# Softmax sums of four heads in one group inside the values, divisors spread by small transfers, output a step later

## What is computed

```python
xn = layernorm(x)                                   # x: 8 x 512 x 128, float32
qkv = xn @ W_qkv + b_qkv                            # 16 heads of 64
attention = softmax(q k^T / sqrt(64))               # per sample and head, 512 x 512
attn = (attention @ v).reshape(n, l, 1024) @ W_out + b_out
# gated recurrence over the 8 samples: f, i = sigmoid(...), g = tanh(...), c = f*c + i*g
h = tanh(xn @ wo.T + c_final @ uo.T + bo)           # c_final is the same for all samples
out = x + attn + h
```

## Time and profile before

| | before |
|---|---|
| runs | 881.68 / 883.38 / 883.47 us |
| the profiled execution | 882.6 us, its span 880.8 us |
| TensorE busy | 856.5 us (97%) |
| VectorE busy | 562.0 us (64%) |
| ScalarE busy | 450.5 us (51%) |
| GpSimd busy | 570.0 us (65%) |
| chain that ended last | TensorE 93%, VectorE 4%, ScalarE 2% |

### The profile page before, as it was taken

One profiled execution on the slowest core, in us unless ns is written; L12 is line 12 of the kernel. 1 busy time (PEld: TensorE's weight loads), 2 busy tenths in 40 slices (PEclk: granted clock), 3 DMA queues, 4 the chain that ended last, 5 costly groups with the idle time before them and its releaser, 6 DMA issues.

```text
span 880.8 us, 14963 instructions
## 1 busy us (share of the span) xinstructions
PE 856.5 (97%) x5431; PEld 541.2 (61%) x5431; DVE 562.0 (64%) x743; ACT 450.5 (51%) x585; POOL 570.0 (65%) x299
## 2 busy tenths in 40 slices
PE   6989999999999999999999999999999999999998
PEld 3655565556666566666666566666666566666553
DVE  6775766656777477755776477755777476755722
ACT  6456465455555255555555255554555255554530
POOL 4637584466777377766777377775777477775764
PEclk9999999999999999999999999999999999999999
DMA  8000000000100010000100010000100010000000
GB/s 239 1 1 1 25 1 1 13 1 6 33 1 13 0 36 0 13 0 0 36 0 12 0 36 0 12 0 0 36 0 12 0 36 0 13 1 1 13 13 12
DMA packets 18636, 13.75 MB, mean 16 GB/s; under 512 B 1299, under 2 KB 16177, under 8 KB 18609
## 3 DMA queue, kind: packets, MB, share of 16 engines
q1 hardware_dynamic: 18560, 13.37, 4.9%
q10 hardware_dynamic: 48, 0.02, 0.0%
HBM read 6.83 MB, written 2.10 MB: 10 GB/s over the span
## 4 chain that ended last, share of the span: by engine, by line
PE 93%; DVE 4%; ACT 2%; issue 1%; DMA 0%; ACTq 0%
PE st L799 20%; PE pv L815 13%; PE misc L815 13%; PE st L732 9%; PE mx L780 8%; PE st L807 6%; PE mx L831 6%; PE mx L825 6%; PE misc L715 3%; PE pv L732 2%; PE misc L732 2%; DVE NM L553 2%; PE pv L715 1%; PE mx L715 1%; ACT probs L387 1%; PE st L696 1%
## 5 line engine op out<-in xcount | busy, mean ns | idle before, releaser
L553 DVE TENSOR_REDUCE NM<-mx 128x2 f32<-128x1024 f32 x256 | 313.9, 1226 | 157.2 <-PE mx L780 157.2
L387 ACT ACTIVATE probs<-st 128x1024 f32<-128x1024 f32 x256 | 256.9, 1027 | 71.5 <-PE st L807 64.5
L272 POOL TENSOR_TENSOR AT<-AT,RD 128x512 f32<-128x512 f32 x63 | 80.7, 1281 | 204.1 <-DVE RD L571 145.9
L280 POOL TENSOR_TENSOR PSUMK<-probs 128x1024 f32<-128x1024 f32 x64 | 153.5, 2398 | 56.8 <-ACT probs L387 56.8
L286 POOL TENSOR_TENSOR PSUMK<-PSUMK,probs 128x1024 f32<-128x1024 f32 x64 | 152.9, 2390 | 6.0
L293 POOL TENSOR_TENSOR PSUMK<-PSUMK,probs 128x1024 f32<-128x1024 f32 x64 | 152.7, 2386 | 6.1
L815 PE MATMUL misc<-probs,VALL 128*64 128x512 f32 x512 | 129.2, 593 | 2.2 <-DVE DL L518 2.2
L815 PE MATMUL pv<-probs,VALL 128*64 128x512 f32 x512 | 125.2, 609 | 0.2 <-DVE RES L524 0.2
L780 PE MATMUL mx<-KH,QH 64*128 64x512 f32 x512 | 106.7, 412 | 7.1 <-DVE NM L553 6.5
L799 PE MATMUL st<-QH,KH 64*128 64x512 f32 x512 | 104.8, 404 | 0.6 <-ACT probs L387 0.6
L799 PE MATMUL st<-QL,KH 64*128 64x512 f32 x512 | 101.7, 392 | 0.0
(11 more groups left out here) (175 smaller groups left out, 1234.2 us busy)
## 6 DMA issues: line engine op xcount, KB each, us to landing
XSH<-XH SPq DMA_DIRECT2D x8, 256.0 KB, 2.4
XSL<-XL SPq DMA_DIRECT2D x8, 256.0 KB, 2.4
RES<-in_L_attn_data_dram SPq DMA_DIRECT2D x8, 256.0 KB, 2.8
out_dram<-RES SPq DMA_DIRECT2D x8, 256.0 KB, 2.3
probs<-in_L_attn_W_qkv_dram SPq DMA_DIRECT2D x3, 512.0 KB, 5.3
AT<-in_L_attn_data_dram SPq DMA_DIRECT2D x2, 512.0 KB, 6.9
MROW<-TM SPq DMA_DIRECT2D x62, 4.0 KB
AT<-in_L_attn_data_dram SPq DMA_DIRECT2D x1, 768.0 KB, 8.1
```

What stands on the lines that cost most here:

```text
L280: nc.gpsimd.tensor_tensor(PSUMK[:, s % 2, :, :], e[:, :, 0, :], e[:, :, 1, :], ALU.add).then_inc(sum_part, 1)
L387: nc.scalar.activation(probs[:, s % 2, :, u, :], st[:, u % 2, :, :], ACT.Exp, scale=SCALE).then_inc(exp_done, 1)
L553: nc.vector.tensor_reduce(NM[:, 0:4 * TB].rearrange("p (h a b) -> p h a b", h=2, a=2)[:, :, s % 2, b], mx[:, :, :], AX.X, ALU.max, negate= ...
```

## The change

- **Four heads as one group.** In merged stretches (stretch 3 of batch 0, all of batches 1 to 6, stretches 0 to 2 of batch 7) the two calls of `sums` go. In their place `four_sums` runs in the middle of the second pair's values: four products of 32 columns each at column positions 0, 32, 64, 96, all into the bank `st[:, 1, 1, :]`. Before it TensorE waits for `k_lo`. The next stretch's `scores(1)`, which writes that bank, waits for `four_turned`.
- **Divisors.** VectorE turns the group once and takes one reciprocal (`invert_four`). At the head of the next stretch SP spreads the reciprocals over the partitions by six small transfers (`spread_divisors`), and at that stretch's end VectorE fills RD with one transpose per pair (`fill_divisors`), behind the copy of the maxima (`take_max`), in stretch 1 ahead of it.
- **Normalisation** on GpSimd comes one stretch later, both pairs together. The first two pairs of a batch are evacuated into a new tile PV2 in the meantime.
- **Output a step later.** `project_out` and `join` move from stretch 0 to stretch 1, `turn_out`, `finish` and the output's transfer from stretch 1 to stretch 2. `recurrence(3)` stays in stretch 0.
- **The end.** Stretch 3 of batch 7 keeps separate sums; GpSimd does the normalisations of stretch 2 between the sums of its two pairs, and the last output projection is cut in pairs 0 to 3, 4 and 5, 6, 7.

```diff
+            def spread_divisors(n, j):
+
+                sp.wait_ge(four_inverted, fours(n, j) - 1)
+                sp.sem_inc(passed_sp, 1)
+                for a in range(2):
+                    for to, of, count in ((0, 0, 32), (32, 0, 64), (96, 32, 32)):
+                        sp.dma_start(RX[to:to + count, a, :],
+                                     R4[HD * a + of:HD * a + of + count, :]).then_inc(d_r, 16)
...
                 for j in range(STRETCHES):
+                    if not first:
+                        spread_divisors(n, j)
...
-                    if j == 1 and not first:
+                    if j == 2 and not first:
                         sp.wait_ge(out_done, n)
...
                     for k in range(2):
-                        first_sum(t + k, s + k)
+                        first_sum(n, j, t + k, s + k, first)
                         second_sum(t + k, s + k)
                         third_sum(t + k, s + k)
...
+                        if last and j == 3 and k == 0:
+                            normalise(n, t - 2, s - 2)
+                            normalise(n, t - 1, s - 1)
+                    if (first and j < 3) or (last and j == 3):
+                        normalise(n, t, s, first)
+                    elif not first:
+                        normalise(n, t - 2, s - 2)
+                        normalise(n, t - 1, s - 1)
...
+            def invert_four(n, j):
+
+                dve.wait_ge(four_done, fours(n, j))
+                nc.vector.transpose(SD[:, :], st[:, 1, 1, :]).then_inc(four_turned, 1)
+                dve.wait_ge(four_turned, fours(n, j))
+                nc.vector.reciprocal(R4[:, :], SD[:, :].rearrange("p (c j) -> p c j", j=32)[:, :, 0]).then_inc(four_inverted, 1)
+
+            def fill_divisors(n, j, t, a):
+
+                dve.wait_ge(d_r, 96 * (fours(n, j) - 1))
+                dve.wait_ge(norm_done, t - 3 + a)
+                nc.vector.transpose(RD[:, a, :].rearrange("p (c j) -> p c j", j=32),
+                                    RX[:, a, :].unsqueeze(2).to_broadcast([P, L // 32, 32])).then_inc(rd_done, 1)
...
-                    if j == 0 and not first:
+                    if not first and j != 1 and coming:
+                        take_max(STRETCHES * n + j + 1)
+                    if not first:
+                        for a in range(2):
+                            fill_divisors(n, j, t, a)
+                    if j == 1 and not first:
                         join(n - 1)
-                    if j == 1 and not first:
+                    if j == 2 and not first:
                         finish(n - 1)
-                    if coming:
+                    if first or j == 1:
                         take_max(STRETCHES * n + j + 1)
...
+            def four_sums(t):
+
+                pe.wait_ge(sum_done, t + 2)
+                for a in range(2):
+                    for h in range(2):
+                        g = 32 * (2 * a + h)
+                        last = nc.tensor.matmul(st[g:g + 32, 1, 1, :], ones[:, 0:32], PSUMK[:, a, h, :], start=True,
+                                                stop=True, tile_position=(0, g))
+                last.then_inc(four_done, 1)
...
                         staged = 32 * n + 64
+                        pe.wait_ge(four_turned, fours(n, j) - 1)
                         scores(n, t, s, 1)
...
                         recurrence(3, n - 1, h_done, N)
+                    if j == 1 and not first:
                         pe.wait_ge(red_done, 4 * (t + 4))
                         pe.wait_ge(norm_done, 8 * n)
                         project_out(mx[:, 1, :])
-                    if j == 1 and not first:
-                        pe.wait_ge(v_evac, 6 + t)
+                    if j == 2 and not first:
+                        pe.wait_ge(v_evac, 6 + t) if ahead else pe.wait_ge(pv_evac, t)
                         turn_out(n - 1)
...
-                    elif j == 1:
+                    elif j == 2:
                         pe.wait_ge(out_done, n)
...
                     pe.wait_ge(exp_done, 4 * t + 8)
-                    if coming:
+                    if merged:
+                        values(n, t + 1, s + 1, (0, 1))
+                        if ahead:
+                            pe.wait_ge(k_lo, t + 6)
+                        four_sums(t)
+                        values(n, t + 1, s + 1, (2, 3))
```

More of the change, by code:

```diff
@@ L65, in build_block @@
         RD = sb("RD", [P, 2, L])
+        SD = sb("SD", [P, L])
+        R4 = sb("R4", [P, L // 32])
+        RX = sb("RX", [P, 2, L // 32])
+        PV2 = sb("PV2", [P, 2, L])
         AT = sb("AT", [P, PAIRS, L])
@@ L142, in build_block @@
         sum_part, sum_done, norm_done, last_norm = sem("sum_part"), sem("sum_done"), sem("norm_done"), sem("last_norm")
-        d_m = sem("d_m")
+        d_m, d_r = sem("d_m"), sem("d_r")
+        four_done, four_turned, four_inverted = sem("four_done"), sem("four_turned"), sem("four_inverted")
         d_xs, d_res, out_rows = sem("d_xs"), sem("d_res"), sem("out_rows")
@@ L149, in wait, with fours, unnormalised @@
                 eng.wait_ge(s, value)
+        def fours(n, j):
+            return STRETCHES * n + j - 2
+        def unnormalised(first, s):
+            return AT[:, s % PAIRS, :] if first or s % PAIRS >= 2 else PV2[:, s % PAIRS, :]
         def placed(n, j):
@@ L266, in _, with normalise, first_sum @@
             standardise(1)
-            def normalise(t, s):
+            def normalise(n, t, s, first=False):
                 pool.wait_ge(rd_done, t + 1)
                 pool.wait_ge(pv_evac, t + 1)
-                nc.gpsimd.tensor_tensor(AT[:, s % PAIRS, :], AT[:, s % PAIRS, :], RD[:, s % 2, :],
+                if not first and s % PAIRS == 0:
+                    pool.wait_ge(o_done, n)
+                nc.gpsimd.tensor_tensor(AT[:, s % PAIRS, :], unnormalised(first, s), RD[:, s % 2, :],
                                         ALU.mult).then_inc(norm_done, 1)
-            def first_sum(t, s):
+            def first_sum(n, j, t, s, first):
                 pool.wait_ge(exp_done, 4 * t + 2)
-                wait(pool, den_done, t - 1)
+                if first:
+                    wait(pool, den_done, t - 1)
+                else:
+                    pool.wait_ge(four_done, fours(n, j) - 1)
                 e = probs[:, s % 2, :, :, :]
@@ L298, in step @@
                     s, t = 2 * j, 8 * n + 2 * j
-                    if not (first and j == 0):
-                        normalise(t - 1, s - 1)
+                    if first and j > 0:
+                        normalise(n, t - 1, s - 1, True)
                     for k in range(2):
-                        first_sum(t + k, s + k)
+                        first_sum(n, j, t + k, s + k, first)
                         second_sum(t + k, s + k)
@@ L374, in evac_pv @@
                 act.wait_ge(pv_done, t + 1)
[L375 to L379, removed]
+                start = isinstance(n, int) and n == 0
+                if start:
+                    act.wait_ge(xt_done, s % PAIRS + 1)
+                elif s in (0, 1):
+                    act.wait_ge(norm_done, t - 7)
+                elif s == 2:
+                    act.wait_ge(o_done, n)
+                nc.scalar.copy(unnormalised(start, s), value_banks[s % 2]).then_inc(pv_evac, 1)
             def exps(t, s, u):
@@ L560, in take_max, with divisors @@
                 nc.vector.tensor_copy(TM[:, :], mx[0:4 * TB, 0, 0:P]).then_inc(tm_done, 1)
-            def divisors(t, s, source):
+            def divisors(t, s, source, count):
                 r = RD[:, s % 2, :]
-                dve.wait_ge(den_done, t + 1)
+                dve.wait_ge(den_done, count)
                 wait(dve, norm_done, t - 1)
                 nc.vector.transpose(r, source).then_inc(den_used, 1)
-                dve.wait_ge(den_used, t + 1)
+                dve.wait_ge(den_used, count)
                 nc.vector.reciprocal(R16[:, :], r.rearrange("p (c j) -> p c j", j=32)[:, :, 0]).then_inc(r16_done, 1)
-                dve.wait_ge(r16_done, t + 1)
+                dve.wait_ge(r16_done, count)
                 nc.vector.transpose(r.rearrange("p (c j) -> p c j", j=32),
                                     R16[:, :].unsqueeze(2).to_broadcast([P, L // 32, 32])).then_inc(rd_done, 1)
+            def invert_four(n, j):
[8 more added lines that the diff above has]
+                                    RX[:, a, :].unsqueeze(2).to_broadcast([P, L // 32, 32])).then_inc(rd_done, 1)
             def join(n, last=False):
@@ L678, in step @@
                         lo_state(s + 2)
-                    divisors(t, s, mx[:, 1, :])
-                    divisors(t + 1, s + 1, mx[:, 0, :] if coming else st[:, 0, 0, :])
+                    if first and j < 3:
+                        divisors(t, s, mx[:, 1, :], t + 1)
+                        divisors(t + 1, s + 1, mx[:, 0, :], t + 2)
+                    elif last and j == 3:
```

(23 more changed lines are left out.)

3 lines of the change are left out of this document (1 added, 2 removed).

## The result

| | before | after |
|---|---|---|
| runs, median (lowest to highest) | 883.42 us (881.68 to 885.71) | 892.13 us (891.88 to 892.39) |
| span of the profiled execution | 880.8 us | 890.5 us |
| TensorE busy | 856.5 us | 846.6 us |
| VectorE busy | 562.0 us | 529.0 us |

The ratio is 1.0097, 95% interval 1.0074 to 1.0120: slower by about 1%. TensorE has 9.9 us less to do, and the span is 9.7 us longer, so its idle time grew by some 20 us.

What follows compares the result with a forecast made beforehand. TensorE was taken as the bound, busy 856.5 of 880.8 us. Terms -16.0 + 9.8 + 11.4 + 0.9 + 0.6 = +6.7 us gave 890.0 us; likeliest range 884.5 to 897.2, 8 in 10 from 879.5 to 901.

Steps and rivals of the forecast that it cites:

- The sums and the group: Merged stretches: one group for two sums saves 0.59 us (bounds 0.33 and 0.80), 27 times, -16.0 us.
- Both choices between far bounds: Group on TensorE: 0.86 us streaming (bounds 0.86 and 1.71) and 0.13 us per change of tile size (0.03 to 0.26).
- the cap: TensorE's moving operand at 614 GB/s would make the group 1.71 us; the prediction set 1,220 GB/s from the trace against it.
- The output projection: Stretch 1, batches 1 to 7: the projection waits 1.4 us for VectorE's last reduction, +9.8 us.
- The output's finish: Stretch 2: second values wait 1.9 us for finish in batches 1 to 6, +11.4 us; in batch 7 +0.9 us.
- The last stretch: End of batch 7: GpSimd's two normalisations between its chains of sums delay its last sum, +0.6 us.
- Edits at nothing: VectorE's turn and reciprocal, the k_lo wait, GpSimd's earlier sum, small transfers, later normalisations and divisors: priced at no cost.
- A sign that did not come: Sign of being right: TensorE's busy time down by some 20 us with the span longer.
- The first two: Rivals on the group: tiles take turns in pairs, 913 us, chance 0.10; change of tile size free, 883 us, chance 0.11.
- The third: Rival in stretch 2: the wait for out_done does not arise, 9.5 us less, 880.6 us; chance 0.09.
- the fourth: Rival: idle time in the 14 new waits lowers the granted clock, 22 us, 912 us; chance 0.05.
- the forecast of 6.7: Whole kernel: sum of all priced terms, +6.7 us against the kernel before.

Runs made afterwards that it cites:

- b1: The kernel before with each of its 64 calls of sums made on four tiles of 32 columns instead of two of 64: 899.44 us, ratio 1.0180.
- e5: The changed kernel with the eight records of each group issued twice in a row: 915.09 us, ratio 1.0369.
- e2: The changed kernel with recurrence(3) and its tanh moved from stretch 0 to stretch 1, ahead of the output projection: 878.44 us, ratio 0.9941.
- e1: The changed kernel with finish in stretch 2 put first, ahead of the copy of the maxima and the fills: 881.31 us, ratio 0.9977.
- e4: The changed kernel with finish in stretch 2 behind the copy of the maxima and ahead of the two fills: 882.53 us, ratio 0.9989.
- e8: The changed kernel with recurrence(3) moved ahead of the output projection in stretch 1 and finish between the two projections' low halves: 868.63 us, ratio 0.9820.
- after_again: The changed kernel timed once more, with no edit, beside the kernel before: 890.67 us, ratio 1.0078.

## Why the prediction was right, point by point

- **The sums and the group.** Forecast 0.59 us saved per group, measured 0.58. Both choices between far bounds held: side by side (b1, e5), 0.27 us for two changes of form where 0.26 were taken (1.71 - 0.86 - 0.58; 0.25 to 0.3 in b1). The 614 GB/s that the Trainium skill (SBUF — State Buffer, the table of paths) gives the moving operand stand there for bf16; for these float32 streams they are no cap: the group streams 8 x 128 x 512 x 4 bytes in 0.99 us, 2,100 GB/s. The prediction's own 1,220 GB/s against the cap was weaker than it looked: it counts both passes of each product, and if a product were read only once, it would be 610. The group settles it, since its four products counted once are still 1,060 GB/s.
- **The output projection.** Forecast 1.4 us late, measured 1.41; taken away by e2.
- **The output's finish.** Forecast 1.9 us in six places, measured 1.87; e1, e4 and e8 give back 1.35, 1.17 and 1.75 of it. In batch 7 0.9 us were forecast, and e1's trace is 0.9 us shorter from that stretch's turn to the end (39.54 to 38.65 us).
- **The last stretch.** Forecast 0.6 us. GpSimd's last sum ended at 878.96, and the second sum started at 879.10, not at 877.73 + 0.86 = 878.59: 0.5 us.

```profile
877.73 1.03 PE L889 MATMUL mx<-PSUMK,ones 128*64 128x512 f32 x4
879.10 1.08 PE L889 MATMUL st<-PSUMK,ones 128*64 128x512 f32 x4 [0.35 <-POOL PSUMK L322]
```

- **Edits at nothing.** The transfers (six issues in 3.76 us), the normalisations, GpSimd's third sum and the wait for `k_lo` left no wait of TensorE in the loop. The fills waited for their transfers once, in the last stretch, and nobody waited for them there.

```profile
330.03 3.76 SPq L201 DMA_DIRECT2D RX<-R  x6
...
862.91 1.30 DVE L624 STREAM_TRANSPOSE RD<-RX 128x512 f32<-128x512 f32 x2 [5.15 <-DMA RX<-R]
```

- **What the sum left out.** It gives -4 x 0.59 + 1.4 + 1.9 = +0.94 us per batch; measured +1.11. Before, two stretches of a batch used the full array at the seam (recurrence with projection, transposes), now three do (recurrence; projection; transposes), so one change of form per batch was added. I had priced those of the group and not this one; by e2's trace it is 0.16 us, the whole difference. Seven batches make 1.1 us.
- **A sign that did not come.** TensorE's busy time was to fall by some 20 us; it fell by 9.9. In a batch of the loop it goes from 99.51 to 97.75 us: 2.87 us are idle, the part of the two waits that is visible, while the batch is 1.11 us longer. It is the idle time that grew by 20 us; the forecast of the time does not rest on this sign.
- **Rivals.** The first two fell with b1. The third had no ground, as `finish` came last in VectorE's queue; e1 made it true by order and took 881.31 us, where the rival had 880.6. For the fourth: the clock stayed at 2.4 GHz through 13 of the 14 waits (1.00 from 166 to 831 us), so idle times of 1.4 and 1.9 us among busy time did not lower it here.

```profile
166.00:831.00 665.00, 645.32 (x4316) 378.75 (x4320) 396.81 (x460) 336.38 (x427) 436.92 (x208) 1.00 0.04 11
```

The last wait lies in stretch 2 of batch 7, where the clock had fallen in the kernel before too. That fall does not follow from the two idle times alone, as the rival had it. In e1 the same two stand there, and the clock stays at 1.00:

```profile
834.72 0.50 PE L844 MATMUL mx<-KH,QH 64*128 64x512 f32 x2 [1.32 <-DVE NM L592]
836.54 0.50 PE L844 MATMUL mx<-KH,QH 64*128 64x512 f32 x2 [1.32 <-DVE NM L592]
```

```profile
837.00:841.00 4.00, 4.00 (x24) 2.19 (x24) 3.08 (x5) 0.00 (x0) 3.86 (x2) 1.00 0.00 0
```

So it does in b1; in the other ten traces it falls there. What decides it is open.

The measured 892.1 us lies 2.1 above the forecast: 1.1 us the change of form left out, and up to 1.8 us of the start, which e1, e2 and after_again did not have. Together they are more than is missing, so other terms came out somewhat smaller or the runs differ by that much. Against the kernel before of its own round, after_again is 7.2 us slower, 0.5 above the forecast of 6.7.

## What to carry to other kernels

When an engine is the bound and an edit removes some of its work, look for what the removed or moved instructions had covered: the recurrence ahead of the projection hid a reduction, the first sum hid `finish`, and the two waits of 1.4 and 1.9 us per batch ate four gains of 0.6. Both could be had back by order alone, with no instruction less: the same cover put ahead of the moved wait, and on an in-order engine the instruction that the bound engine waits for placed ahead of those that nobody waits for yet. And price each change of form on TensorE: at 0.13 us each, four of them nearly cancel what one merged group gains.

## What the runs showed of the hardware that I had not expected

- Four column tiles of 32, 128 rows deep, with four different float32 streams, run fully side by side: eight records in 0.86 us of streaming, as four records on two tiles do. I had given that nine chances in ten; no row of before had shown more than two.
- A change of tile form costs TensorE about 0.13 to 0.2 us, and part of it falls on the second record of the new form. From the maxima (64-row tiles) to the values (column tiles) of stretch 2 in the trace of before, the starts are 340.96, 341.28 and 341.76, where 0.23 and 0.43 are the paces: 0.09 and 0.05 late. From the maxima to the recurrence (full array) they are 286.73, 287.05 and 287.39, where 0.23 is the pace of both: 0.09 and 0.11 late. The two changes of a group amid values cost 0.25 to 0.3.
- The granted clock is lowered for differing times, or not at all, in two places: the start (the second turn of the maxima comes at 34.5 us with it at 1.00 and at 37.1 us with it at 0.91), and stretch 2 of batch 7 (1.25 us between e1 and the changed kernel). Differences of 1 to 3 us between kernels are better read from the batches of the loop: from 40 to 800 us it is 1.00 in all twelve traces.
